# GpSimd's gathers held to three batches ahead of TensorE in a graph layer

## What is computed

```python
xn = _layernorm(x, axis=-1)
x = x + _L0_gnn_ref(xn, edge_index, ...) + _L0_mix_ref(xn[None], ...)[0]
x = x + _L0_ffn_ref(_layernorm(x, axis=-1)[None], ...)[0]
```

## Time and profile before

| | |
|---|---|
| median of 3 runs (3394.37 to 3410.11) | 3405.5 us |
| the profiled execution | 3382.15 us |
| its span, first to last instruction | 3380.7 us |
| mean granted TensorE clock | 0.809 |
| TensorE busy (matmul / weight load) | 2141.0 us (63%) / 1625.9 us (48%) |
| VectorE / ScalarE busy | 1423.6 us (42%) / 955.7 us (28%) |
| GpSimd busy | 1607.6 us (48%), 1661 gathers of 963 ns |
| DMA | 340.31 MB, mean 101 GB/s |

### The profile page before, as it was taken

The page is one execution under the profiler, slowest core; times in us unless marked ns, Lnnn a source line. Parts: engine busy times, 40 slices in busy tenths (PEclk is TensorE's granted clock), DMA queues, the critical chain, the costliest instruction groups (busy, mean ns, idle before and its releaser), DMA issues.

```text
span 3380.7 us, 35327 instructions
## 1 busy us (share of the span) xinstructions
PE 2141.0 (63%) x10858; PEld 1625.9 (48%) x10858; DVE 1423.6 (42%) x3244; ACT 955.7 (28%) x2221; POOL 1607.6 (48%) x1679
## 2 busy tenths in 40 slices
PE   1147667657766775565465454654555557999998
PEld 0135445545444553343343333433333346999997
DVE  7612222334444443332333323333333335777777
ACT  4512222222222221111111111111111114656565
POOL 1256666665555555666566665666566640000000
PEclk9978788878777777767767777677777778999999
DMA  6633333333333333333333333333333322222221
GB/s 210 215 101 115 112 111 110 91 102 106 100 97 100 98 93 103 98 103 98 98 101 100 103 101 96 100 101 102 98 98 103 103 70 77 75 63 68 74 74 58
DMA packets 205191, 340.31 MB, mean 101 GB/s; under 512 B 33118, under 2 KB 151131, under 8 KB 205115
## 3 DMA queue, kind: packets, MB, share of 16 engines
q0 software_dynamic: 80160, 219.14, 22.6%
q1 hardware_dynamic: 124538, 119.81, 11.1%
q10 hardware_dynamic: 416, 0.39, 0.1%
HBM read 288.01 MB, written 51.20 MB: 100 GB/s over the span
## 4 chain that ended last, share of the span: by engine, by line
PE 41%; another core or an unknown queue 34%; issue 9%; ACT 7%; DVE 7%; DMA 1%; ACTq 1%; SPq 0%; DVEq 0%
PE pd L1290 8%; PE pd L1094 6%; PE pa L1275 4%; PE pc L1275 4%; PE pa L1244 3%; PE pd L995 2%; PE pa L1243 2%; PE pd L1105 2%; PE pd L1087 2%; PE pd L1134 1%; PE pc L1005 1%; PE pc L1145 1%; PE pd L1108 1%; PE pd L1109 1%
## 5 line engine op out<-in xcount | busy, mean ns | idle before, releaser
L672 POOL DMA_INDIRECT ring<-xn_table,idxb x1661 | 1598.8, 963 | 1150.4 <-issue 633.2
L1244 PE MATMUL pa<-ring,ohh 128*128 128x257 f16 x1661 | 472.0, 305 | 76.4 <-issue 76.2
L1243 PE MATMUL pa<-ring,ohh 128*128 128x256 f16 x1661 | 469.9, 304 | 75.0 <-issue 65.9
L1087 PE MATMUL pd<-work,KS_s 128*128 128x256 f32 x196 | 107.8, 652 | 472.3 <-DVE work L1548 395.5
L1290 PE MATMUL pd<-parts 128*128 128x256 f32 (+1 forms) x1568 | 312.2, 282 | 1.8 <-DVE parts L1747 1.8
L1087 PEld LDWEIGHTS pd<-work,KS_s 128*128 128x128 f32 x196 | 49.7, 313 | 489.0 <-DVE work L1548 404.6
L1244 PEld LDWEIGHTS pa<-ring,ohh 128*128 128x128 f16 x1661 | 179.8, 108 | 197.0 <-issue 121.8
L1094 PE MATMUL pd<-mats,work 128*128 128x256 f32 x784 | 260.1, 463 | 0.9 <-DVE work L1530 0.9
L1290 PEld LDWEIGHTS pd<-parts 128*128 128x128 f32 (+1 forms) x1568 | 253.1, 188 | 10.3 <-DVE parts L1747 2.4
L1504 DVE TENSOR_TENSOR ohh<-pc,edges 128x512 f16<-128x512 f32 (+1 forms) x307 | 214.2, 718 | 98.4 <-PE pa L1244 64.6
L768 ACT ACTIVATE ring<-pa 128x257 f32<-128x257 f32 x196 | 75.4, 385 | 620.1 <-remote 313.5
(11 more groups left out here) (205 smaller groups left out, 3726.1 us busy)
## 6 DMA issues: line engine op xcount, KB each, us to landing
ring<-xn_table,idxb POOLq DMA_INDIRECT x1661
yT<-in_x SPq DMA_DIRECT2D x48, 512.0 KB
xn_table<-ring SPq DMA_DIRECT2D x24, 512.0 KB, 5.4
x_rows<-work SPq DMA_DIRECT2D x48, 256.0 KB
y_rows<-work SPq DMA_DIRECT2D x48, 256.0 KB
work<-y_rows SPq DMA_DIRECT2D x24, 512.0 KB, 4.3
work<-x_rows SPq DMA_DIRECT2D x24, 512.0 KB, 3.7
out<-work SPq DMA_DIRECT2D x24, 512.0 KB, 3.1
```

Source lines behind the costliest of these rows:

```text
L672: pool.indirect_dma_start(out=msgs[:, k, 0:PARTS * D], out_offset=None, in_=xn_table[:, :], in_offset=bass.IndirectOffsetOnAxis(ap=idxb[:, ...
L1087: ins = mm(pd[:, 0, c * BN:(c + 1) * BN], KS_s[:, c, :], pq[:, c * BN:(c + 1) * BN], start=True, stop=True)
L1243: mm(pa[:, t % 2, 0:D], oh[:, slot, :], msgs[:, k, 0:D], start=begins, stop=False, skip_group_check=True)
L1244: ins = mm(pa[:, t % 2, 0:D + 1], oh[:, slot, :], msgs[:, k, D:2 * D + 1], start=False, stop=ends, skip_group_check=True)
```

## The change

The number of batches that GpSimd may be ahead goes from 8 to 3. Nothing else differs; the ring keeps its 34 slots, and the same instructions are issued.

```diff
@@ -66,7 +66,7 @@
     BATCH = [(0, 4), (4, 8), (8, 13), (13, 17), (17, 21), (21, 25), (25, 30), (30, 34)]
     NBT = len(BATCH)
     SLOTS = TB // 2
-    AHEAD = NBT
+    AHEAD = 3
 
     DELAY = 10
     XB = 4
```

## The result

The changed kernel took 3344.0 us (median of 4 runs, 3339.7 to 3349.6) against 3402.25 us (3394.4 to 3410.1) of the kernel before in the same visit: ratio 0.983, 95% interval 0.980 to 0.986, 58 us less. The forecast was 3374, 28 us less: sign right, gain half of what came. **But the sign held only on some chips.** The later visits went to chips numbered 0, 1, 5, 9 and 12 (that of the first visit has no number on record). Chip 12 was visited once, so whether the difference belongs to the chip or to that visit stays open; no visit showed both kinds of time.

A forecast was written before the change was run, and what follows sets the result against it. GpSimd's gather stream with its two pauses a block was taken as the pace; -26 + 18 + 12 - 35 = -31 us, from the 3405.5 us median to 3374 us, range 3295 to 3480.

The forecast's parts named there:

- (1) Landing: Gathered rows reaching TensorE, 6.6 us after a batch's first gather begins: covered by the two batches between, cost 0.
- (2) The start: Blocks 0 and 1: first run of 42 gathers shortens to 13 to 17, L723 answered 34 us earlier; -26 us.
- (3) Blocks 2 to 9: Pace goes from 49.7 to 52 us a block with shorter runs and pauses; +18 us, bounds 0 and +65.
- (4) Blocks 10 to 19: TensorE and its chains bound; answers up to one gather (1.25 us) later in 20 halves; +12 us, bounds 0 and +40.
- (5) The late blocks: 27 blocks from 20 on: wait for indices goes, 51.9 to 50.6 us a block; -35 us, bounds -62 and +60.
- (6) The end: Behind the last gather nothing is touched, no gather coming after 2760: 0 us.
- One sign that I had named: Profile after: GpSimd's waits on TensorE's L1244 would be several times as long as before.
- Rival (b): Much faster: with short runs late signals vanish, one 3.5 us pause, 46.1 us a block; -211 us, 3195 us; chance 0.10.
- Rival (a): Slower: TensorE's short and key chains meet the cap, 54 us a block; +77 us, 3482 us; chance 0.38.
- the rule of the Trainium skill: Rule against the change: a shorter run-ahead gains nothing, start and late-block gains would be 0, sum +30 us.

The follow-up runs named there:

- distance 2: Changed kernel with two batches ahead in place of three (AHEAD = 2), chip 5: 3505.9 us, ratio 1.029 against the kernel before.
- Experiment 1: Kernel before with the cap of three batches in blocks 0 and 1 only, whole ring afterwards: 3376.4 us, ratio 1.0016.
- experiment 2: Kernel before, whole ring, with ScalarE making the indices of batches 3 and 4 one step earlier: ratio 0.982.
- experiment 3: Kernel before, whole ring, with GpSimd waiting from block 1 on before every second batch until the previous batch has landed: ratio 0.982.
- 8: Kernel before, whole ring, with each gather moving 512 bytes in place of 1 KB per partition: 3399.2 us against 3401.3.
- 9: Kernel before, whole ring, with a 128x128 memset on GpSimd ahead of each batch: ratio 0.997 on chip 9, 1.0091 on chip 12.

## Why the prediction was right in sign and half in size

The mean of the three profiles after less the mean of the two before, on chips that hold signals up, against the terms. The two means are not of the same chips, so a few us in each are scatter:

- **(1) Landing, 0.** Wrong as told: TensorE waits 441 us for gathers, in most blocks, not once. I had said that this would make the forecast wrong. It didn't. My reading, argued and not tested: the waits stand where TensorE had waited for ScalarE's and VectorE's answers before (L1087 395.5 to 139.3 us), while GpSimd sets the pace. With distance 2 the same wait, 711 us, does cost.
- **(2) The start, -26:** measured 96 - 120 = -24. Right, and the prompt answer of L723 too.
- **(3) Blocks 2 to 9, +18:** +15 (408 and 405; 430 once). Right. Experiment 1 shows that terms 2 and 3 belong together and come to nearly nothing.
- **(4) Blocks 10 to 19, +12:** -4, within the scatter of this stage (612 and 625 us of before). The 16 us between them are a good part of what the forecast missed. The later answers that I had priced are there (L790 is idle for 178.3 us in these blocks, before for 157.4 and 133.8), but the stage doesn't lengthen; why not stays open.
- **(5) The late blocks, -35: the term that was mis-sized.** It covers block 20 too. Blocks 21 to 46 gained 64 us (1376 to 1312), block 20 lost 10: -54 in place of -35. The pace after was forecast at 50.6 us a block and measured 50.6, 50.2 and 50.5 in blocks 21 to 46. The error is in the base: I took one execution, whose 27 blocks took 1403 us, and the second profile of the same kernel has 1428, so the mean is 12 us above my base. The other 7 us are that the 27 blocks after took 1361 us, where the term gave 1403 - 35 = 1368. That my window held the short block 20 shifted the pace from 52.5 to 51.9 and explains none of this. The first two profiles alone give -39. The reason held: GpSimd's waits for indices disappeared, and removing them alone (experiment 2) gives about the same 1.8%.
- **(6) The end, 0:** blocks 47 and 48 lost 12 us. Their short time before came, like block 20's, from rows stored ahead.

Sum: -24 + 15 - 4 + 10 - 64 + 12 = -55 where the terms had -31; the medians of the first visit say -58, those of chips 1 and 0 -55 and -46. The steps that failed are the sizes of term 5 (-35, measured -54) and term 4 (+12, measured -4); term 6 goes 12 us the other way. That the first two profiles alone differ by 32.5 us, as forecast, was chance.

One sign that I had named came out the other way: GpSimd's waits on L1244 were to be several times as long, and fell from 168.1 to 87.6 us. GpSimd's time under "issue" rose from 633.2 to 834.5 us meanwhile, the longest from 8.3 to 12.7, so these labels don't tell how often the cap was met.

On the pattern itself: that late signals grow out of unbroken runs I had taken from two places of the trace, and experiment 3 bears it out; 8 and 9 rule out the bytes and the missing of other instructions. The trace also records when each semaphore was raised: that of the L1078 which ends at 1674.64 was raised at 1687.27 us, 0.03 us before L790 starts. So the raising is late, and ScalarE answers it at once. Rival (b), that short runs make them vanish, came halfway: with runs mostly of 12 to 17, L790 still waits 203 to 221 us on unplaced signals. Its price was far too small: I gave 3195 us for a kernel without late signals, and chip 12 shows 2861 us. The double stage, in which I saw no gain, falls there from 625 to 451 us. Rival (a), the slower one, came true at distance 2 and on chip 12, by the mechanism it named as far as the stages tell: GpSimd stops whenever TensorE stands. Its place was wrong: the double stage lost most, not the late blocks.

And the rule of the Trainium skill (DMA: Bandwidth & Descriptors, Rules for kernel authors: issue a DMA early, wait on it late), which I had set aside, agrees with chip 12: keeping more gathers ahead is worth 92 us. The other chips show 46 to 58 us the other way. I argued from one trace as if it were the kernel; it was the kernel on one sort of chip (or visit).

## What to carry to other kernels

A long unbroken stream of GpSimd gathers can delay what other engines wait for, and the profile shows it as waits on an unknown source in a program on one core; shorten the runs, or take what GpSimd needs out from behind the delayed instruction, and measure on more than one chip, since where the delay is missing the same cap costs 3%. Take the base of a term from more than one execution: two of the same kernel differed by 25 us in the 27 late blocks, nearly as much as the whole forecast. And set two profiles against each other only after their own medians.

## What the runs showed of the hardware

- On chips 0, 1, 5 and 9 and on that of the first visit, TensorE's L1078 signals come late when they are sent more than 7 us into an unbroken run of gathers (43 of 43 in the first profile of before, 26 of 26 in that of after). Those sent more than 9 us in come 1.3 to 2.9 us after the run's last gather has ended; those sent 7.1 us in often come 0.5 us before it. In the first 5.1 us all 22 come at once. The gathers themselves start every 1.25 us either way.
- This depends neither on the bytes (512 or 1024 a partition: 408.6 and 379.2 us of L790's waits, same chip) nor on a 0.2 us instruction between gathers. Pauses in which the gathers land, 2.8 us each (212.8 / 77), end it. What holds the signals up stays open.
- The traces differ in one thing more: for 5635 instructions of TensorE, VectorE and ScalarE that raise a semaphore, the three profiles on chip 12 record 5723 to 5734 raisings, those of all other visits 4324 to 4561. Whether several raisings arrive as one there, or only their records are missing, no run tells.
- On chip 12 it doesn't occur at all, though there all 1661 gathers are one run: the same program and the same 1.25 us, 2861 us against 3372 to 3402, 15 to 16% less. Of the two levels of TensorE's clock (1.2 and 2.4 GHz) the upper one was granted more of the time there: 0.91 against 0.78 of full speed in blocks 10 to 19, in which TensorE stood still less. Which came first no run tells; that the start differs too (83 against 120 us for blocks 0 and 1, with L723 at 163.9 in place of 201.6) speaks for the signals.
